# Two buffers for v and o, q projected beside the attention, output projection in one block, FFN a tile later

## The reference

```python
q = relu(x @ Wq) * 64 ** -0.5        # (row, 64 heads, 64)
k = relu(x @ Wk);  v = x @ Wv        # the same shape
kv  = einsum('bsid,bsjd->bsdj', k, v)     # over the heads of one row
out = einsum('bsid,bsdj->bsij', q, kv)
out = out / (einsum('bsid,bsd->bsi', q, k.sum(axis=2)) + 1e-6)
x = layernorm(x + out.reshape(b, s, 4096) @ Wo + bo)
# FFN: fp4_linear quantises input and weight in blocks of 16 along the last axis
gate, up = fp4_linear(x, w_gate), fp4_linear(x, w_up)    # 128 -> 352
x = layernorm(x + fp4_linear(silu(gate) * up, w_down))   # 352 -> 128
```

## Time and profile before

| | |
|---|---|
| median of three runs | 2814.91 us |
| profiled execution | 2816.36 us, of which 2814.6 us are the span of the trace |
| granted PE clock, mean | 0.921 |
| PE, DVE, ACT, POOL busy | 2230.0, 2325.8, 1601.0, 1603.7 us |
| from one output projection to the next | 41.90 us (starts at 1395.60 and 1437.50) |

### The profile page before, as it was taken

How to read it: one execution, slowest core, us unless ns; L and a number is a source line. 1 busy time by engine, 2 the same in 40 slices (tenths; PEclk the granted TensorE clock), 3 DMA queues, 4 the chain that set the end, 5 groups by cost and what they waited for, 6 DMA issues and landing times.

```text
span 2814.6 us, 94862 instructions
## 1 busy us (share of the span) xinstructions
PE 2230.0 (79%) x37963; PEld 2110.7 (75%) x37963; DVE 2325.8 (83%) x4452; ACT 1601.0 (57%) x2442; POOL 1603.7 (57%) x1746
## 2 busy tenths in 40 slices
PE   2787888888888888888888888888878878878864
PEld 2777787787777777777777778778778778778764
DVE  8588888888888898898888898898888898898884
ACT  2565565565565565565565565565565565565561
POOL 5365565565565565565565564565565565565563
PEclk8899999999999999999999999999999999999986
DMA  4445645644644644644644644644654654654652
GB/s 130 107 91 107 129 93 103 129 95 102 130 95 100 130 99 97 130 100 95 130 101 94 130 105 91 130 106 90 130 107 92 127 111 89 127 111 88 127 110 46
DMA packets 356966, 303.13 MB, mean 108 GB/s; under 512 B 281734, under 2 KB 307270, under 8 KB 356422
## 3 DMA queue, kind: packets, MB, share of 16 engines
q1 hardware_dynamic: 356934, 302.67, 51.1%
HBM read 17.38 MB, written 4.19 MB: 8 GB/s over the span
## 4 chain that ended last, share of the span: by engine, by line
DMA 25%; DVE 23%; PE 22%; issue 18%; SPq 8%; POOL 3%; DVEq 1%; ACT 0%; POOLq 0%; ACTq 0%
PE ps L356 16%; DMA o_st<-o_st 10%; DMA o_st<-swap 10%; DVE o L669 6%; SPq L246 5%; DVE q L648 4%; SPq L241 3%; POOL o_st L923 3%; DVE x L786 3%; PE ps L319 2%; PE ps L321 2%; PE ps L320 2%; DVE xq L687 2%; DMA swap<-v_st 1%; DMA v_st<-swap 1%
## 5 line engine op out<-in xcount | busy, mean ns | idle before, releaser
L923 POOL TENSOR_TENSOR o_st<-o,o_st 128x512 bf16<-128x512 f32 x512 | 610.0, 1202 | 402.9 <-ACT o_st L501 402.9
L356 PE MATMUL ps<-w_o,o_st 128*128 128x128 bf16 x6144 | 524.6, 263 | 330.8 <-DMA o_st<-swap 330.8
L356 PEld LDWEIGHTS ps<-w_o,o_st 128*128 128x128 bf16 x6144 | 514.5, 157 | 342.7 <-issue 337.2
L648 DVE SCALAR_TENSOR_TENSOR q<-ps,ks 128x1024 f32<-128x1024 f32 x256 | 311.2, 1216 | 330.3 <-ACT ks L528 321.3
L917 POOL TENSOR_TENSOR q_nat<-q,q_nat 128x512 bf16<-128x512 f32 x512 | 577.9, 1162 | 9.8 <-ACT q_nat L490 9.8
L319 PE MATMUL ps<-v_st,q_bd 128*128 128x66 bf16 x4096 | 439.0, 198 | 89.9 <-DVE o L669 80.7
L319 PEld LDWEIGHTS ps<-v_st,q_bd 128*128 128x128 bf16 x4096 | 414.9, 114 | 115.2 <-DVE o L669 102.6
L496 ACT COPY q_bd<-q_nat 64x2048 bf16<-64x2048 bf16 x256 | 484.6, 1893 | 4.7
L501 ACT CAST o_st<-o 128x512 bf16<-128x512 f32 x512 | 312.1, 622 | 275.3 <-DVE o L669 275.2
L320 PE MATMUL ps<-v_st,q_bd 128*128 128x66 bf16 x4096 | 435.8, 198 | 0.0
L321 PE MATMUL ps<-v_st,q_bd 128*128 128x66 bf16 x4096 | 434.8, 196 | 0.0
(11 more groups left out here) (137 smaller groups left out, 5832.9 us busy)
## 6 DMA issues: line engine op xcount, KB each, us to landing
q_bd<-q_nat SPq DMA_DIRECT2D x256, 256.0 KB, 5.4
swap<-v_st SPq DMA_DIRECT2D x128, 288.0 KB, 5.2
v_st<-v_st SPq DMA_DIRECT2D x128, 288.0 KB, 5.0
v_st<-swap SPq DMA_DIRECT2D x128, 288.0 KB, 5.2
swap<-o_st SPq DMA_DIRECT2D x128, 256.0 KB, 2.8
o_st<-o_st SPq DMA_DIRECT2D x128, 256.0 KB, 5.0
o_st<-swap SPq DMA_DIRECT2D x128, 256.0 KB, 5.1
x_in<-in_L_attn_x SPq DMA_DIRECT2D x64, 64.0 KB, 3.3
```

The lines of the kernel that those rows point to most:

```text
L356: last = nc.tensor.matmul(TB0[:, 0:DIM], omat[:, lo, :, j], womat[:, lw, j, :], start=(j == 0 and i == 0), stop=(j == HALF - 1 and i == 2))
L648: nc.vector.scalar_tensor_tensor(out=q32[:, c % QR, :].rearrange("p (e t) -> p e t", t=T), in0=slot_cols(("q", c)), scalar=0.0, in1=ks[:, ...
L923: nc.gpsimd.tensor_tensor(lo, o32[:, g % OR, :].rearrange("p (s b e) -> p s b e", b=2, e=HALF), hi, ALU.subtract).then_inc(s_olo, 1)
```

## The change

The new order of the projections on PE is v0 to v3, k0 to k3, then q0, and from there q1, q2, q3 between attention groups; the output projection of tile n-2 stands as one block at the end of the iteration. v and o have two buffers each, taken by the parity of the tile, so the loop body holds two iterations. The first layer norm, its quantiser, gate and up belong now to tile n-3 and the down projection with the second layer norm to tile n-4. `q32` and `o32` have 2 places instead of 4. `q_lo` stands between the `o_lo` of its groups on POOL. One of the four `q_stay` is now on POOL, as a product with 1.0 (64 partitions x 2048 elements). `o_st` is laid out so that PE reads columns 8 bytes apart instead of 64, which cuts each `o_hi` and `o_lo` into two instructions of 128x256. The quantiser is a scaling, a bitwise and, an addition and a subtraction of a large number (rounding by the fp32 format). One TENSOR_SCALAR of each layer norm has become a SCALAR_TENSOR_TENSOR.

```diff
-QR = 4
+QR = 2
-OR = 4
+OR = 2
-USES = ([("k", c) for c in range(NC)]
-        + [u for c in range(NC) for u in (("q", c), ("out", 2 * c), ("out", 2 * c + 1))]
-        + [("v", c) for c in range(NC)])
+USES = ([("v", c) for c in range(NC)] + [("k", c) for c in range(NC)]
+        + [u for c in range(NC) for u in (("q", c), ("out", 2 * c), ("out", 2 * c + 1))])
...
-        v_st = sb("v_st", [P, 2 * 2 * S * VS], BF16)
-        o_st = sb("o_st", [P, 2 * 2 * S * HALF], BF16)
+        v_st = [sb(f"v_st{i}", [P, 2 * 2 * S * VS], BF16) for i in range(2)]
+        o_st = [sb(f"o_st{i}", [P, 2 * 2 * S * HALF], BF16) for i in range(2)]
...
@@ PE, iteration n, with e = n - 4, b = n - 3, m = n - 2 @@
+                    project(n, par, "v", 0)
+                    pe.wait_ge(s_hq, e + 1)
...
+                    for c in range(NC):
+                        project(n, par, "k", c)
+                if back:
+                    pe.wait_ge(s_xq, b + 1)
...
+                    nc.tensor.transpose(TB1[:, 0:T], xq[:, :], ident[:, :]).then_inc(s_xqps, 1)
+                if front:
+                    project(n, par, "q", 0)
+                    pe.wait_ge(s_tree, (n + 1) * 3)
...
+                    for i in range(len(WO_PARTS)):
+                        wo_part(par, i)
...
@@ DVE @@
+            def normalise(dst, src, sc, out_sem):
+                nc.vector.scalar_tensor_tensor(out=blocks(dst), in0=blocks(src), scalar=BELOW_ONE,
+                                               in1=per_block(sc, src), op0=ALU.mult, op1=ALU.mult).then_inc(out_sem, 1)
+            def top_bits(dst, src, out_sem):
+                nc.vector.tensor_tensor(dst.bitcast(I32), src.bitcast(I32),
+                                        consts[:, 2:3].bitcast(I32).to_broadcast([P, src.shape[1]]),
+                                        ALU.bitwise_and).then_inc(out_sem, 1)
...
+                    dve.wait_ge(s_rs1, b + 1)
+                    nc.vector.scalar_tensor_tensor(out=x1[:, :], in0=r1[:, :], scalar=mv1[:, 0:1],
+                                                   in1=rs1[:, 0:1].to_broadcast([T, DIM]), op0=ALU.subtract,
+                                                   op1=ALU.mult).then_inc(s_x1, 1)
...
@@ POOL @@
+                if back:
+                    rstd(b, s_agg1, mv1, ve1, rs1, s_ve1, s_rs1)
+                if attend:
...
+                    nc.gpsimd.tensor_tensor(qbd[64:128, 1, :, 1, HALF:DH, :].rearrange("p k e s -> p k (e s)"),
+                                            held, consts[64:128, 4:5].unsqueeze(2).to_broadcast([64, NK, HALF * SB]),
+                                            ALU.mult).then_inc(s_qstay_p, 1)
...
+                for c in range(NC):
+                    if attend:
+                        o_lo(o, par, 2 * c)
+                    if front:
+                        q_lo(n, c)
+                    if attend:
+                        o_lo(o, par, 2 * c + 1)
+                if back:
+                    pool.wait_ge(s_hs, b + 1)
+                    nc.gpsimd.tensor_tensor(blocks(h[:, :]), blocks(h[:, :]), per_block(hsc[:, 0, :], h[:, :]),
+                                            ALU.mult).then_inc(s_hq, 1)
```

More of the change, by code:

```diff
@@ L26 @@
 BF16 = mybir.dt.bfloat16
+I32 = mybir.dt.int32
 ALU = mybir.AluOpType
@@ L385, in iteration, with wo_part @@
-            def iteration(n):
-                front, more, attend, mid, back = parts(n)
-                m, b = n - 2, n - 3
+            def wo_part(par, i):
+                j0, j1 = WO_PARTS[i]
+                for j in range(j0, j1):
+                    for t, (lo, lw) in enumerate(((0, 0), (0, 1), (1, 0))):
+                        last = nc.tensor.matmul(TB0[:, 0:DIM], omat[par][:, lo, j // EB, :, j % EB], womat[:, lw, j, :],
+                                                start=(j == 0 and t == 0), stop=(j == HALF - 1 and t == 2))
+                if j1 == HALF:
+                    last.then_inc(s_y, 1)
@@ L388, in iteration @@
+            def iteration(n, par):
+                o, m, b, e = n - 1, n - 2, n - 3, n - 4
+                front, more, attend, mid, back, end = (live(n, i) for i in (0, -1, 1, 2, 3, 4))
+                first = isinstance(n, int) and n == 0
                 if front:
                     pe.wait_ge(s_xlo, n + 1)
-                    first = isinstance(n, int) and n == 0
-                    if first:
-                        pe.wait_ge(s_wlo["k"], 1)
-                    for c in range(NC):
-                        if first and c == SLOTS - 1:
-                            pe.wait_ge(s_ffnw, 1)
-                        if first and c == SLOTS:
-                            transpose_down_weights()
-                        project(n, "k", c)
@@ new lines, in o_hi, with iteration @@
+            def o_hi(o, par, g):
+                act.wait_ge(s_read["out"], o * NG + g + 1)
+                src = o32[:, g % OR, :].rearrange("p (s b f e) -> p b f s e", b=2, f=NE, e=EB)
+                for a in range(2):
+                    last = nc.scalar.copy(ost[1 - par][:, 0, :, a, g * G:(g + 1) * G, :], src[:, a])
+                last.then_inc(s_ohi, 1)
+            def iteration(n, par):
+                o, m, b, e = n - 1, n - 2, n - 3, n - 4
+                front, more, attend, mid, back, end = (live(n, i) for i in (0, -1, 1, 2, 3, 4))
+                if front and isinstance(n, int) and n < 2:
+                    act.wait_ge(s_clear, 1 if n == 0 else 3)
+                if front:
+                    v_hi(n, par, 0)
@@ L539, in iteration @@
                     if front:
                         q_hi(n, c)
-                    if back and c == 1:
-                        act.wait_ge(s_hps, b + 1)
-                        for i, (k0, kn) in enumerate(DOWN):
-                            last = nc.scalar.copy(hqT[0:kn, i, :], TB1[0:kn, i * T:(i + 1) * T])
-                        last.then_inc(s_hqT, 1)
-                    if attend:
-                        o_hi(o, 2 * c)
-                    if front and c == NC - 1:
-                        v_hi(n, 0)
@@ L550, in iteration @@
-                    if attend:
-                        o_hi(o, 2 * c + 1)
-                    if mid and c == 0:
-                        act.wait_ge(s_x1, m + 1)
-                        nc.scalar.activation(xa[:, :], x1[:, :], ACT.Abs).then_inc(s_xabs, 1)
-                        nc.scalar.activation(xsgn[:, :], x1[:, :], ACT.Sign).then_inc(s_xsgn, 1)
-                if more:
-                    act.wait_ge(s_xps, n + 2)
-                    nc.scalar.copy(xk[:, 0, :], TB0[:, 0:T]).then_inc(s_xhi, 1)
@@ L559, in iteration @@
[L559 to L569 removed]
+                    if attend:
+                        o_hi(o, par, 2 * c + 1)
```

816 lines of the change are left out of this document (391 added, 425 removed).

## The result

The changed kernel takes 3180.36 us, the median of four runs (3173.04 to 3182.16), beside 2813.93 us for the kernel before on the same chip (2811.44 to 2816.94, four runs). The ratio is 1.130, with a 95% interval from 1.1275 to 1.1319: slower by 13%. The forecast was 3040 us and slower; the time lies at the upper end of the range of 2760 to 3180, 0.4 us past it.

The account below looks back on a forecast made before the run. The prediction took a chain of handovers with DVE nearly full as the bound. 61 tiles of 46.2 us (22.0 + 17.1 + 5.3 + 1.8) and 221 at start and end gave 3041, called 3040 us; range 2760 to 3180.

Parts of the forecast that it names:

- V: The start of v0, PE's first product in the predicted iteration; `hq` was to come 3.6 us after it.
- the sum: The predicted period of one tile: 22.0 + 17.1 + 5.3 + 1.8 = 46.2 us, giving 3041 us in all.
- v0 to q0: First half of the iteration, from the start of v0 to that of q0: predicted 22.0 us.
- both my bounds: POOL's new 64x2048 copy was to take between 4.4 and 5.03 us; 4.4 was used.
- the lock: DVE's `x1`, with two SBUF inputs, waits for POOL's copy to end: 1.7 us lost, bounds 0 and 1.7.
- q0 to the projection: Second half, from q0 to the output projection, paced by POOL: 17.1 us, plus 1.8 for the clock.
- the 1.8 us for the clock: PE starts q0 at low clock after 4.5 us idle; q0 and the sum slow down: 1.8 us, bounds 0 and 4.4.
- The loop of twice the length: The loop body of two iterations was to cost nothing that could be priced; no row showed a wait for code.
- B: Rival: no lock on `x1` and no clock loss at q0; 42.7 us a tile, 2826 us, near no change; chance 0.20.
- C: Rival: POOL's split `o_lo` is cheap, deciding from about 1.0 us each; 40.2 us a tile, 2673 us; chance 0.14.
- D: Rival: gaps on PE keep the clock at 0.50 over the output projection too; 50.2 us a tile, 3283 us; chance 0.08.
- E: Rival: 7 us of DVE work and 5 us of wait go; about 34 us a tile, 2300 us; chance 0.03.

Follow-up runs that it names:

- e2: The changed kernel with no loop, all 68 iterations written out: 3114.54 us, ratio 1.1065 to the kernel before.
- e4: The changed kernel with PE's transpose of `xq` moved behind out0, the first attention group: 2973.97 us, ratio 1.058 to the kernel before.
- e5: The changed kernel with POOL's 64x2048 copy first in the iteration, ahead of the first layer norm: 3142.38 us, ratio 1.117 to the kernel before.
- e1: The kernel before with a loop body of two iterations instead of one, nothing else: 2897.66 us, ratio 1.030.
- e11: The changed kernel with four edits, as in e10, and POOL's order in a chunk `o_lo`, `o_lo`, `q_lo`: 2908.23 us, ratio 1.0342 to the kernel before.
- e10: The changed kernel without loop, `xq`'s transpose behind out0, POOL's copy first, `hq`'s product ahead of the last chunk's products: 2912.92 us, ratio 1.0334 to the kernel before.
- e9: The kernel before with the new o layout (split casts) and the shorter quantiser, order unchanged: 2733.12 us, ratio 0.9706.
- e12: The changed kernel with a loop body of four iterations instead of two: 3152.0 us, ratio 1.1194 to the kernel before.

## Why the prediction was right, and which term it lacked

**The path.** The profile shows the five places that the prediction named: the gap of 4.55 us between k3 and `xq`'s transpose, released by POOL (4.5 predicted); the clock of 0.50 behind it; `x1` at a mean of 1.235 us, released at the end of POOL's copy; PE behind v0 waiting for `hq`, which comes 3.7 us behind V (1600.07 to 1603.78; 3.6 predicted); the projection at 5.3 us and full clock. The period without the hole of a jump is 46.48, for 46.2 in the sum; with no loop at all (e2) it is 47.12. e4 shows that the first two of them together are the main cost: 206 us for moving one transpose.

**The terms.** v0 to q0 was 22.0 and is 21.72, which is nearer than the terms are: behind a jump nothing waits for `hq`, and without a loop it is 22.33. POOL's copy takes 3.60 us, under both my bounds (4.4 and 5.03), which takes 0.8 us out of what stands behind it on POOL and shortens the lock: `x1` loses 0.9 us to it where the sum had 1.7, and e5 gives 0.6 us a tile back. Against it DVE's 128x352 forms stand at 0.92 and 1.00 us instead of 0.53 (the shortest of each takes 0.52 and 0.51), and I had priced a loss there at nothing. They run while POOL does `o_lo` and `q_lo` and read two SBUF tensors, so I take them for the same lock; it wasn't tried. q0 to the projection was 18.9 with the clock and is 19.45: an `o_lo` pair takes 1.42 us instead of 1.25, inside the bounds of 1.15 to 1.6, and out7 hangs on four of them, 0.7 us. Of the 1.8 us for the clock q0 alone shows 1.25 (24 products in 2.76 us instead of 1.51). Start and end together are 231 us for 221 (3176.9 less 61 x 48.30).

**The term that was missing.** "The loop of twice the length costs nothing that I can price; no row shows a wait for code": this step failed. It costs 1.82 us a tile in front of v0, of which the bare wait for `hq` would have taken 0.6: e2 gives 66 us back, and e1 shows the same with nothing else changed. The trace of before had a row that bears on it, which I didn't use: 0.38 MB of instructions in 2.8 ms. The 68 iterations of e2, written out, took 4.90 MB, so 0.38 MB is some five iterations' worth (an estimate), and the body that ran 60 times was not fetched anew each time. The Trainium skill bears on it in "Runtime: NRT & Kernel Launch", section "Instruction fetch mechanics": code is fetched ahead in sequence, and a taken branch to a target outside a window of two pages waits for a fetch. The traces agree with 4.90 MB at no gap without a loop, and 28 gaps of 3.5 us with it. They do not agree with a window of two pages, if a page is the skill's block of 256 instructions: one iteration has 1186 of PE's instructions (37963 products and as many loads over 64 tiles), and yet the jumps back to it in the kernel before left no gap in front of k0. The same section of the Trainium skill gives PE room for 2048 instructions. By that figure one body fits and two don't, an estimate that could have been made ahead and that e1 bears out.

Without a loop the period is 47.12 us, 0.9 over the sum, and with it 48.30, against 48.5 at the forecast's upper end. That the time still came out at the end of the range is luck: no term of the sum or of the range stood for this cost.

**The difference of 138 us** between the profiled 3178.7 and the sum's 3041 is then 61 x (1.82 - 0.28 + 0.55) = 128, and 10 at start and end.

**The rivals.** B (no lock, no clock loss) and C (cheap `o_lo`) fall with the rows above: each condition is refuted, C's by 1.42 us against the 1.0 from which it decides. D falls with the clock of 1.00 over the projection; a little of what it feared shows in e11. E was half right about its parts, and wrong about the sum: the layout and the quantiser gain 81 us, but in the old order. The two buffers did what they were for, since no engine waits for the o swap any more; but the new order cost more than that wait was worth. With the four costly places mended (e10) the mean iteration is still 43.94 us, against 40.93 for the old order with the same two parts (e9). PE's waits, as the profile lists them, sum to 650.7 us in e10 and 516.0 in e9: one wait for the o swap (362.4 us in e9) has become many smaller ones, for `xq` 153.3, for `o` 107.8, for the sum of k 85.6 us. Which of them could be taken out was not tried, so what makes up these last 3 us stays open.

**The best version** is e9: 2733.12 us, 2.9% under the kernel before.

## What to carry to other kernels

Before a loop body is doubled (two buffers by parity are the usual reason), count the instructions of one engine in it and look at what the instruction queue has moved: a few tenths of a MB for the whole run means that the body is held, and where it wasn't held each jump cost some 2 to 3 us of the time here (83 us over 29 in e1, 66 over 28 in e2, 28 over 15 in e12). Taking a wait of 5 us out of a ring wasn't worth a move that put another engine's last result in front of PE's next products: ask of each border in the new order whose result comes last there, and put that reader one group later. And try the parts that don't need the new order on the old one: two of them were worth 3% here.

## What the runs showed of the hardware

- Each of the 28 jumps back to a body of 2373 PE instructions held PE for 3.5 us on average, in front of v0; a body of 1186 and straight code of 4.9 MB left no such gap.
- DVE's TENSOR_SCALAR of 128x8, a form that reads one tensor, was held until a POOL instruction of 3.60 us had ended (1.62 us instead of 0.14).
- POOL multiplies 64x2048 bf16 in 3.60 us; 128x512 fp32 into bf16 takes 1.20.
- At full clock a weight load of 128 columns takes 150 ns (median over all tiles) where they are 64 bytes apart, 113 ns at 8 bytes and 98 ns side by side, and the products start 64, 56 and 56 ns apart. At the low clock they start 107 ns apart in either layout. The load's median over the whole run before is 157 ns, but that mixes both levels. These are the loads of the projection before, in all, from 1443.50 on (clock 1.00) and up to 1442.50 (0.50); then of the projection now; then of k now, which stand side by side (ns least/median/most, and for the last a group with its mean):

```profile
L356 PEld LDWEIGHTS ps<-w_o,o_st x6144: 136/157/183, 133.1 to 2787.5; 128*128 128x128 bf16 x199
L356 PEld LDWEIGHTS ps<-w_o,o_st x39: 136/151/160, 1443.4 to 1446.1; 128*128 128x128 bf16 x39
L356 PEld LDWEIGHTS ps<-w_o,o_st x48: 144/168/168, 1437.5 to 1442.4; 128*128 128x128 bf16 x48
```

```profile
L359 PEld LDWEIGHTS ps<-w_o,o_st x6144: 111/113/147, 149.5 to 3154.4; 128*128 128x128 bf16 x199
```

```profile
L336 PEld LDWEIGHTS ps<-xT,w_k 128*128 128x128 bf16 x2048 | 200.6, 98 | 0.0
```
